# Weight maxima spread over the partitions by TensorE transposes instead of by GpSimd

## The chip, the cores and the metric

The kernel is one program on one core of a Trainium2 chip. The metric is the device time of one execution in microseconds; less is better. TensorE does the matrix products, VectorE (DVE) and ScalarE (ACT) the elementwise work and the reductions along a row, GpSimd (POOL) some elementwise work, and SyncE (SP) issues most of the transfers. A tensor in the on-chip memory has 128 partitions (rows); a reduction along a row is ordinary work for DVE, one over the partitions is not.

## The reference

One layer with two parallel branches on the normalised input, added to the input:

```python
xn = layernorm(x)                       # x: 4 sequences x 2048 x 512
# linear attention, 64 heads of 8
q = softmax(exp(beta) * heads(xn @ Wq.T + bq)); k = softmax(exp(beta) * heads(xn @ Wk.T + bk))
v = heads(xn @ Wv.T + bv)
kv = cumsum(einsum('zsD,zsd->zsDd', k, v)); kn = cumsum(k)
att = (einsum('zsD,zsDd->zsd', q, kv) / sum(q * kn)) @ Wo.T + bo
# one product whose inputs are rounded to fp8 (e4m3)
ffn = dequantised(fp8(clip(xn / input_scale))) @ (weight_fp8 * weight_scale).T + bias
out = x + att + ffn
```

## The kernel before

The 2048 positions are cut into 64 steps of 32 positions of all four sequences, which fill 128 partitions. Every engine runs its own list of work, in order, and waits on semaphores for the others. In iteration i of the main loop (`body`) TensorE makes keys, queries and values of step i, scores and attention of step i-1 and the output product of step i-2. A product in single precision is made of three in half precision: each of the five weight matrices is kept as a high part and a low part in float16 (`w_hi`, `w_lo`), scaled by a power of two that comes from the largest absolute value of the matrix.

The setup ahead of the loop makes these parts, in the order K, Q, V, F (the fp8 product's), O:

- SP loads the weights; DVE takes the largest absolute value of each partition (`largest`, L823, into one column of `amax`). GpSimd takes the maximum over the partitions and leaves it in all of them (`partition_all_reduce`, L444 for K, Q and V, L447 for F and O, into `amax_all`). DVE turns it into powers of two (`powers`, L828 to L832, `w_mult` at L867), and counts `mult_ready`.
- TensorE transposes each matrix in four chunks of four 128x128 transposes (`transpose_weights`, L1107) into seven banks of PSUM. ACT writes the high part of a chunk (`high_parts`, L567), DVE the low part (`low_parts`, L839), and then the bank is free for a later chunk.
- ACT issues the loads of the five biases at L587 (`b_loaded`). GpSimd, after both `b_loaded` and `mult_ready`, scales the biases (L453 for K and Q, which counts `bias_ready`, L456 for V) and adds the two output biases (L460, `obias_ready`).
- TensorE primes two banks (L1118, `primed`); ACT then writes the biases into the banks of keys and queries (L595, L596); only then may TensorE start keys and queries of step 0, `keys(0)` and `queries(0)`.
- Inside iteration 0, behind `queries(0)`, stand the transposes of F and O (`late_weights`, on TensorE, ACT and DVE), and behind them `values(0)`. At its end ACT sums the absolute low part of F (L581, `lo_summed`), GpSimd shares the result over the partitions (L462, `lo_total`), and TensorE reads it before iteration 2: if it is zero, as it is for a weight that is exact in fp8, every step leaves out four products with the low part of F.

At the end of iteration i ACT writes the biases for the keys of i+1 (L547, L550). The input of step i+1 is normalised by DVE (L645), split by ACT and GpSimd (L479, L402) and transposed by a transfer of SP (L324) into `xT`. In iteration 1 (`fold`) DVE adds a folded bias at L808 before `values(1)` may start; `shift` (L670, L674) is DVE's first work on the keys. On SP the load of the input of step 4 is queued behind the transposing transfers of step 1.

Of the kernel before, what the change touches and what calls it, by code (L numbers as in the profile page):

```python
# [27 lines left out]
ALU = mybir.AluOpType  # L28
ACT = mybir.ActivationFunctionType
AX = mybir.AxisListType  # L30

P = 128
# [26 lines left out]
MATRICES = 5  # L59
# [63 lines left out]
def build(nc, x, wq, bq, wk, bk, wv, bv, wo, bo, beta, wf, bf, in_scale, w_scale, const, out):  # L123
# [3 lines left out]
    with ExitStack() as ctx:  # L127
        def sb(name, shape, dt=F32):
            return ctx.enter_context(nc.sbuf_tensor(name, shape, dt))
# [4 lines left out]
        def sem(name):  # L134
            return ctx.enter_context(nc.semaphore(name))
# [26 lines left out]
        lo_sum, lo_total = sb("lo_sum", [P, 1]), sb("lo_total", [P, 1])  # L162

# [70 lines left out]
        amax_ready, amax_shared = sem("amax_ready"), sem("amax_shared")  # L234
        chain = sem("chain")
# [133 lines left out]
        def _(pool):  # L369
# [67 lines left out]
            for n in range(2):  # L437
# [5 lines left out]
            pool.wait_ge(amax_ready, 3)  # L443
            gp.partition_all_reduce(amax_all[:, 0:MO], amax[:, 0:MO], P, bass.bass_isa.ReduceOp.max)\  # L444
                .then_inc(amax_shared, 1)
            pool.wait_ge(amax_ready, MATRICES)
            gp.partition_all_reduce(amax_all[:, MO:], amax[:, MO:], P, bass.bass_isa.ReduceOp.max)\  # L447
                .then_inc(amax_shared, 1)

            pool.wait_ge(b_loaded, 16 * 5)  # L450
            pool.wait_ge(mult_ready, 1)
            for m in (MK, MQ):
# [8 lines left out]
            pool.wait_ge(lo_summed, 1)  # L461
            gp.partition_all_reduce(lo_total[:, :], lo_sum[:, :], P, bass.bass_isa.ReduceOp.max)\  # L462
                .then_inc(lo_shared, 1)
# [139 lines left out]
        def _(dve):  # L603
# [168 lines left out]
            def body(i, last_weights=None, fold=False):  # L772
# [33 lines left out]
                if fold:  # L806
                    dve.wait_ge(bvo_done, 1)
                    v.scalar_tensor_tensor(bias[:, 3, :], vo_ps[:, :], out_dn[:, :], bias[:, 3, :],  # L808
                                           ALU.mult, ALU.add).then_inc(fold_ready, 1)
# [11 lines left out]
            def largest(m):  # L821
                dve.wait_ge(w_loaded[m], 16)
                v.tensor_reduce(amax[:, m:m + 1], w_nat[m][:, :, :], AX.XY, ALU.max,  # L823
                                apply_absolute_value=True).then_inc(amax_ready, 1)

# [21 lines left out]

# [16 lines left out]
            quantise(Step(0, 0))  # L864
            dve.wait_ge(amax_shared, 1)
            powers(slice(0, MO))
            v.tensor_copy(w_mult[:, 0:MO], w_scale_up[:, 0:MO]).then_inc(mult_ready, 1)  # L867
            dve.wait_ge(mult_ready, 1)
            largest(MF)
            low_parts(MK)  # L870
            largest(MO)
            low_parts(MQ)
            low_parts(MV)
            dve.wait_ge(amax_shared, 2)
            link(v.tensor_tensor(amax_all[:, MF:], amax_all[:, MF:], abs_scales[:, :], ALU.mult))
# [12 lines left out]
            dve.wait_ge(obias_ready, 1)  # L888
# [7 lines left out]
        def _(pe):  # L896
# [195 lines left out]
            def transpose_weights(m):  # L1092

                if m == MO:
                    pe.wait_ge(wo_ordered, 1)
                else:
                    pe.wait_ge(w_loaded[m], 16)
                for c in range(KC):
                    n = turn.index(m) * KC + c
                    if last_in_bank(n) is not None:  # L1100
                        pe.wait_ge(wl_ready, last_in_bank(n) + 1)
                    for oc in range(KC):
                        src = (wo_sorted if m == MO else w_nat[m])[:, oc, c * P:(c + 1) * P]
                        dst = bank_of(n)[:, oc * P:(oc + 1) * P]
                        if m == MV:
                            dst = bank_of(n).rearrange("p (g q u f) -> p q u g f", g=GP, q=KC, f=J * DH)[:, oc]
                        last = transpose(dst, src, ident)  # L1107
                    last.then_inc(wt_done, 1)

            def late_weights():  # L1110
                transpose_weights(MF)
                transpose_weights(MO)

# [48 lines left out]
```

## Time and profile before

| | |
|---|---|
| time, median of 3 runs (lowest to highest) | 1186.12 us (1186.01 to 1186.84) |
| time of the profiled execution | 1187.5 us |
| span of that execution, first to last instruction | 1185.7 us |
| mean granted clock of TensorE | 0.982 |
| busy: TensorE, VectorE, ScalarE, GpSimd | 94%, 82%, 76%, 39% |

A profile shows one execution. Busy time is given for each engine; idle time of an engine is put down to what released the instruction behind it ("issue" is time in which the profile shows nothing that it waited for). The setup and the first two iterations take the first 101 of the 1185.7 us; the rest is the steady loop.

### The profile page before, as it was taken

To read this page: it belongs to the slowest core of one execution; us is meant where nothing else is said; L and a number is where in the kernel's file an instruction comes from. 1 tells how busy PE (TensorE), PEld (TensorE's weight loads), DVE (VectorE), ACT (ScalarE), POOL (GpSimd) and SP (SyncE) were. 2 spreads that over 40 slices of the span, in tenths; PEclk is the share of its full clock that TensorE was granted. 3 is DMA by queue.
4 is the path that set the end of the run, shared out by engine and by line. 5 is a ranking of instruction groups with operands and counts; after the bars stand their busy time and mean duration, and the time that the engine had idled before them with its cause. 6 is when DMAs were issued, how large, how long until landed. Compare 5 with 4: busy or idle time off the path is not lost.

```text
span 1185.7 us, 57406 instructions
## 1 busy us (share of the span) xinstructions
PE 1115.6 (94%) x24098; PEld 627.9 (53%) x24098; DVE 967.9 (82%) x1968; ACT 899.3 (76%) x1933; POOL 463.6 (39%) x717
## 2 busy tenths in 40 slices
PE   1458999999999999999999999999999999999996
PEld 1224555555555555555555555555555555555553
DVE  4648888888888888888888888888888888888883
ACT  0356787888878787878888888878887878787873
POOL 3133434443433444444434443443434443434420
PEclk9689999999999999999999999999999999999999
DMA  8312434544554455445445554454333343333331
GB/s 242 27 43 69 93 87 91 87 97 87 81 94 91 87 84 97 92 82 87 95 88 86 92 95 85 81 98 93 85 83 94 88 89 86 97 87 86 73 76 48
DMA packets 156468, 104.38 MB, mean 88 GB/s; under 512 B 111968, under 2 KB 128480, under 8 KB 156256
## 3 DMA queue, kind: packets, MB, share of 16 engines
q1 hardware_dynamic: 155536, 99.76, 41.1%
q8 instruction: 193, 3.16, 1.1%
q10 hardware_dynamic: 720, 1.31, 0.3%
q14 instruction: 19, 0.16, 0.0%
HBM read 40.20 MB, written 16.78 MB: 48 GB/s over the span
## 4 chain that ended last, share of the span: by engine, by line
PE 91%; issue 4%; DVE 2%; DMA 2%; POOL 1%; SPq 0%; ACT 0%; POOLq 0%; DVEq 0%
PE s_ps L941 11%; PE a_ps L1045 7%; PE vo_ps L907 5%; PE k_ps L1001 5%; PE k_ps L907 5%; PE k_ps L918 5%; PE k_ps L922 5%; PE k_ps L920 5%; PE vo_ps L911 5%; PE vo_ps L909 5%; PE q_ps L909 5%; PE q_ps L911 5%; PE k_ps L911 5%; PE k_ps L909 5%; PE q_ps L907 5%; PE a_ps L1030 4%
## 5 line engine op out<-in xcount | busy, mean ns | idle before, releaser
L496 ACT ACTIVATE st_pairs<-st_run 32x144 f32<-32x144 f32 x1008 | 331.0, 328 | 11.9
L422 POOL TENSOR_TENSOR w_own<-vp,cst 128x576 f32<-128x576 f32 x126 | 141.9, 1147 | 314.0 <-DVE vp L754 314.0
L556 ACT ACTIVATE q_heads<-qT,cst 128x512 f32<-128x512 f32 x256 | 164.1, 711 | 4.9 <-DVE qT L770 3.8
L698 DVE TENSOR_TENSOR att<-s_ps,cst 128x512 f32<-128x512 f32 x256 | 163.5, 680 | 0.3 <-PE s_ps L941 0.3
L941 PE MATMUL s_ps<-q_heads,w_own 64*64 64x128 f32 x4096 | 141.6, 275 | 1.3 <-DVE att L698 1.3
L409 POOL TENSOR_TENSOR y_sum<-y,y_magic 128x512 f32<-128x512 f32 x64 | 81.6, 1274 | 151.6 <-DVE y_magic L656 151.6
L941 PEld LDWEIGHTS s_ps<-q_heads,w_own 64*64 64x64 f32 x4096 | 110.6, 132 | 55.2 <-issue 55.0
L538 ACT ACTIVATE w_own<-kT,cst 128x512 f32<-128x512 f32 x128 | 85.5, 715 | 61.3 <-DVE kT L738 61.3
L402 POOL TENSOR_TENSOR x_split<-xn,x_split 128x512 f16<-128x512 f32 x64 | 74.6, 1165 | 137.6 <-ACT x_split L479 130.4
L479 ACT ACTIVATE x_split<-xn 128x512 f16<-128x512 f32 x64 | 40.3, 630 | 99.2 <-DVE xn L645 99.2
L907 PE MATMUL k_ps<-w_hi,xT 128*128 128x512 f16 x256 | 99.0, 387 | 17.1 <-DMA xT<-x_split 12.3
L907 PE MATMUL vo_ps<-w_hi,xT 128*128 128x512 f16 x256 | 97.7, 382 | 1.2 <-DVE bias L808 1.2
L909 PE MATMUL k_ps<-w_lo,xT 128*128 128x512 f16 x256 | 98.2, 384 | 0.0
L911 PE MATMUL k_ps<-w_hi,xT 128*128 128x512 f16 x256 | 98.0, 383 | 0.0
L918 PE MATMUL k_ps<-w_hi,ah 128*128 128x512 f16 x256 | 97.0, 379 | 0.6 <-DVE al L761 0.6
L754 DVE TENSOR_TENSOR vp<-vo_ps,vp 128x512 f32<-128x512 f32 x64 | 44.3, 692 | 64.7 <-PE vo_ps L911 64.7
L909 PE MATMUL q_ps<-w_lo,xT 128*128 128x512 f16 x256 | 97.0, 379 | 0.0
L911 PE MATMUL q_ps<-w_hi,xT 128*128 128x512 f16 x256 | 97.0, 379 | 0.0
L907 PE MATMUL q_ps<-w_hi,xT 128*128 128x512 f16 x256 | 97.0, 379 | 0.0
L909 PE MATMUL vo_ps<-w_lo,xT 128*128 128x512 f16 x256 | 97.0, 379 | 0.0
L911 PE MATMUL vo_ps<-w_hi,xT 128*128 128x512 f16 x256 | 97.0, 379 | 0.0
L922 PE MATMUL k_ps<-w_hi,al 128*128 128x512 f16 x256 | 97.0, 379 | 0.0
(144 smaller groups left out, 2272.6 us busy)
## 6 DMA issues: line engine op xcount, KB each, us to landing
v_groups<-vp SPq DMA_DIRECT2D x512, 36.0 KB, 3.3
x_in<-L_attn_x SPq DMA_DIRECT2D x64, 256.0 KB
x_res<-L_attn_x SPq DMA_DIRECT2D x64, 256.0 KB
out<-o_sb SPq DMA_DIRECT2D x64, 256.0 KB
w_own<-L_attn_Wk SPq DMA_DIRECT2D x1, 1024.0 KB, 12.7
w_own<-L_attn_Wq SPq DMA_DIRECT2D x1, 1024.0 KB, 14.7
w_own<-L_attn_Wv SPq DMA_DIRECT2D x1, 1024.0 KB, 16.5
att<-L_ffn_weight_fp SPq DMA_DIRECT2D x1, 1024.0 KB, 18.2
```

The lines of the kernel that those rows point to most:

```text
L422: last = gp.tensor_tensor(v_pairs[:, c].rearrange("p h w -> p (h w)"), vp[:, t.parity].rearrange("p h w -> p (h w)"), pair_mask[:, c:c + 1 ...
L496: last = sc.activation(st_pairs[TOK * b:TOK * (b + 1), to, u::J, :, b % SP, :], st_run[TOK * u:TOK * (u + 1), b // SP, :, b % SP, :, :], A ...
L538: last = sc.activation(k_pairs[:, i.parity, :, c, :], kT[:, :, :], ACT.Copy, scale=pair_mask[:, c:c + 1])
L556: last = sc.activation(q_heads[:, i.parity, :, j, :], qT[:, i.parity, :, :], ACT.Copy, scale=head_mask[:, j:j + 1])
L698: v.tensor_tensor(att[:, c % 2, 4 * (c // 2):4 * (c // 2) + 4, :, :] .rearrange("p g j s -> p (g j) s"), s_ps[:, DM * (c % 2):DM * (c % 2 ...
L907: mm(bank[:, :], xT[:, t.parity, 0, c, :], w_hi[:, m, c, :], start=(c == 0 and not seeded), stop=False, skip_group_check=seeded)
L909: mm(bank[:, :], xT[:, t.parity, 0, c, :], w_lo[:, m, c, :], start=False, stop=False, skip_group_check=seeded)
L911: last = mm(bank[:, :], xT[:, t.parity, 1, c, :], w_hi[:, m, c, :], start=False, stop=(c == KC - 1), skip_group_check=seeded)
L918: mm(bank[:, :], ah[:, j, :], w_hi[:, MO, j, :], start=(j == 0 and not rest), stop=False, skip_group_check=rest)
L922: last = mm(bank[:, :], al[:, j, :], w_hi[:, MO, j, :], start=False, stop=(j == J - 1), skip_group_check=rest)
L941: last = mm(s_ps[SP * TOK * gp:SP * TOK * (gp + 1), DM * n + P * q:DM * n + P * (q + 1)], k_pairs[rows, t.parity, g, :, :].rearrange("p c ...
L1045: last = mm(a_rows[TOK * u:TOK * (u + 1), n, h, :, j, :], att[:, n, J * h + u, j, :], v_groups[:, t.parity, :, n, J * h + u, j, :], start= ...
```

## The change

The three uses of `partition_all_reduce` on GpSimd go. For the weights, TensorE transposes the n columns of `amax` into n rows of `t_ps`, DVE takes the maximum of each row and writes it 128 times into a row (`spread_top`), and TensorE transposes back (`turn_top`), so that each partition has all n maxima; DVE copies them to `amax_all`. The first exchange stands on TensorE ahead of the eighth chunk of the transposes of Q, on DVE behind `quantise(0)`. The second stands on TensorE at the head of `late_weights`, behind `queries(0)`; on DVE at the place of the old wait, now behind the two maxima of F and O, which are moved behind all low parts of K, Q and V. The sum of the low parts is transposed into a row of partition 0 at the end of `late_weights`, and DVE takes its maximum (`largest_low`). DVE's wait for the added output biases is moved from before iteration 0 to L808 in iteration 1.

```diff
--- before.py
+++ after.py
@@ -160,6 +160,7 @@
         up_product = sb("up_product", [P, 1])
         lo_abs = w_own[2][:, 0:KC // 2, :].rearrange("p c d -> p (c d)").bitcast(F16)
         lo_sum, lo_total = sb("lo_sum", [P, 1]), sb("lo_total", [P, 1])
+        top, top_row = sb("top", [P, 1]), sb("top_row", [P, P])
 
         x_in = sb("x_in", [P, SLOTS, DM])
         x_res = sb("x_res", [P, 2, DM])
@@ -232,6 +233,7 @@
         c_loaded, b_loaded, m_loaded = sem("c_loaded"), sem("b_loaded"), sem("m_loaded")
         w_loaded = [sem(f"w_loaded{n}") for n in range(MATRICES)]
         amax_ready, amax_shared = sem("amax_ready"), sem("amax_shared")
+        amax_turned, top_spread, lo_turned = sem("amax_turned"), sem("top_spread"), sem("lo_turned")
         chain = sem("chain")
         mult_ready, beta_exped, in_inv_ready = sem("mult_ready"), sem("beta_exped"), sem("in_inv_ready")
         wo_ordered, lo_summed, lo_shared = sem("wo_ordered"), sem("lo_summed"), sem("lo_shared")
@@ -440,13 +442,6 @@
             root(Step(0, 0))
             low_input(Step(0, 0))
             rounding(Step(0, 0))
-            pool.wait_ge(amax_ready, 3)
-            gp.partition_all_reduce(amax_all[:, 0:MO], amax[:, 0:MO], P, bass.bass_isa.ReduceOp.max)\
-                .then_inc(amax_shared, 1)
-            pool.wait_ge(amax_ready, MATRICES)
-            gp.partition_all_reduce(amax_all[:, MO:], amax[:, MO:], P, bass.bass_isa.ReduceOp.max)\
-                .then_inc(amax_shared, 1)
-
             pool.wait_ge(b_loaded, 16 * 5)
             pool.wait_ge(mult_ready, 1)
             for m in (MK, MQ):
@@ -458,9 +453,6 @@
                              w_scale_up[:, MV:MV + 1, None, None].to_broadcast([P, J, 2, DM // J // 2]), ALU.mult)\
                 .then_inc(bias_ready, 1)
             gp.tensor_tensor(bias[:, 3, :], bias[:, 3, :], bias[:, 4, :], ALU.add).then_inc(obias_ready, 1)
-            pool.wait_ge(lo_summed, 1)
-            gp.partition_all_reduce(lo_total[:, :], lo_sum[:, :], P, bass.bass_isa.ReduceOp.max)\
-                .then_inc(lo_shared, 1)
             iterations(pool, body)
 
 
@@ -805,6 +797,7 @@
                     mask_scores(t, 3)
                 if fold:
                     dve.wait_ge(bvo_done, 1)
+                    dve.wait_ge(obias_ready, 1)
                     v.scalar_tensor_tensor(bias[:, 3, :], vo_ps[:, :], out_dn[:, :], bias[:, 3, :],
                                            ALU.mult, ALU.add).then_inc(fold_ready, 1)
                 if d.exists():
@@ -823,6 +816,17 @@
                 v.tensor_reduce(amax[:, m:m + 1], w_nat[m][:, :, :], AX.XY, ALU.max,
                                 apply_absolute_value=True).then_inc(amax_ready, 1)
 
+            def spread_top(n, done):
+
+                dve.wait_ge(amax_turned, done)
+                link(v.tensor_reduce(top[0:n, :], t_ps[0:n, 0:P], AX.X, ALU.max))
+                v.tensor_copy(top_row[0:n, :], top[0:n, 0:1].to_broadcast([n, P])).then_inc(top_spread, 1)
+
+            def largest_low():
+
+                dve.wait_ge(lo_turned, 1)
+                v.tensor_reduce(lo_total[0:1, :], t_ps[0:1, 0:P], AX.X, ALU.max).then_inc(lo_shared, 1)
+
             def powers(part):
 
                 link(v.tensor_scalar(amax_all[:, part], amax_all[:, part], 1e-18, 1e18, ALU.max, ALU.min))
@@ -844,7 +848,7 @@
                 dve.wait_ge(mult_ready, 2)
                 low_parts(MF)
                 low_parts(MO)
-
+                largest_low()
 
             dve.wait_ge(m_loaded, 48)
             link(v.reciprocal(in_rec[:, :], scal[:, 1:2]))
@@ -862,16 +866,20 @@
             magic(Step(0, 0))
             largest(MV)
             quantise(Step(0, 0))
+            spread_top(MO, 1)
             dve.wait_ge(amax_shared, 1)
+            link(v.tensor_copy(amax_all[:, 0:MO], t_ps[:, P:P + MO]))
             powers(slice(0, MO))
             v.tensor_copy(w_mult[:, 0:MO], w_scale_up[:, 0:MO]).then_inc(mult_ready, 1)
             dve.wait_ge(mult_ready, 1)
-            largest(MF)
             low_parts(MK)
-            largest(MO)
             low_parts(MQ)
             low_parts(MV)
+            largest(MF)
+            largest(MO)
+            spread_top(MATRICES - MO, 2)
             dve.wait_ge(amax_shared, 2)
+            link(v.tensor_copy(amax_all[:, MO:], t_ps[:, P:P + MATRICES - MO]))
             link(v.tensor_tensor(amax_all[:, MF:], amax_all[:, MF:], abs_scales[:, :], ALU.mult))
             powers(slice(MO, MATRICES))
 
@@ -885,7 +893,6 @@
             link(v.tensor_tensor(q_exp_scale[:, :], exp_beta[:, :], w_scale_dn[:, MQ:MQ + 1], ALU.mult))
             link(v.tensor_tensor(k_exp_scale[:, :], exp_beta[:, :], w_scale_dn[:, MK:MK + 1], ALU.mult))
             dve.wait_ge(c_loaded, 16)
-            dve.wait_ge(obias_ready, 1)
             statistics(Step(0, 2))
             body(Step(0, 0), last_weights=late_weights)
             body(Step(0, 1), fold=True)
@@ -1097,6 +1104,8 @@
                     pe.wait_ge(w_loaded[m], 16)
                 for c in range(KC):
                     n = turn.index(m) * KC + c
+                    if last_in_bank(n) == 0:
+                        turn_top(slice(0, MO), MO, 1)
                     if last_in_bank(n) is not None:
                         pe.wait_ge(wl_ready, last_in_bank(n) + 1)
                     for oc in range(KC):
@@ -1107,9 +1116,20 @@
                         last = transpose(dst, src, ident)
                     last.then_inc(wt_done, 1)
 
+            def turn_top(part, ready, done):
+
+                n = part.stop - part.start
+                pe.wait_ge(amax_ready, ready)
+                transpose(t_ps[0:n, 0:P], amax[:, part], ident).then_inc(amax_turned, 1)
+                pe.wait_ge(top_spread, done)
+                transpose(t_ps[:, P:P + n], top_row[0:n, :], ident[0:n, 0:n]).then_inc(amax_shared, 1)
+
             def late_weights():
+                turn_top(slice(MO, MATRICES), MATRICES, 2)
                 transpose_weights(MF)
                 transpose_weights(MO)
+                pe.wait_ge(lo_summed, 1)
+                transpose(t_ps[0:1, 0:P], lo_sum[:, :], ident).then_inc(lo_turned, 1)
 
             pe.wait_ge(c_loaded, 16)
             for m in (MK, MQ, MV):
```

## Rows read from the trace of the kernel before

**Rows 1.** Windows: stretch, length, busy PE, PEld, DVE, ACT, POOL (instructions), clock, DMA, GB/s.
```profile
118.40:136.00 17.60, 17.60 (x397) 9.84 (x383) 14.75 (x30) 13.94 (x31) 5.92 (x6) 1.00 0.40 87
```

**Rows 2.** Timeline of POOL: start, length (us), instruction, idle time before it and releaser.
```profile
32.71 0.38 POOL L444 PARTITION_ALL_REDUCE amax_all<-amax  x1 [7.36 <-issue]
41.37 0.37 POOL L447 PARTITION_ALL_REDUCE amax_all<-amax  x1 [8.27 <-DVE amax L823]
48.51 2.03 POOL L453 TENSOR_TENSOR bias<-bias,w_scale_up 128x512 f32<-128x512 f32 x2 [6.77 <-issue]
...
67.08 0.38 POOL L462 PARTITION_ALL_REDUCE lo_total<-lo_sum  x1 [14.32 <-ACT w_own L581]
74.74 1.14 POOL L402 TENSOR_TENSOR x_split<-xn,x_split 128x512 f16<-128x512 f32 x1 [7.28 <-issue]
```

**Rows 3.** Timeline of DVE in the setup, 25 to 54 us.
```profile
25.39 0.43 DVE L664 TENSOR_SCALAR xq_rows<-y_round 128x512 f16<-128x512 f32 x1 [0.59 <-POOL y_round L413]
33.13 0.17 DVE L828 TENSOR_SCALAR amax_all<-amax_all 128x3 f32<-128x3 f32 x1 [7.32 <-POOL amax_all L444]
...
34.15 2.29 DVE L823 TENSOR_REDUCE amax<-att 128x1 f32<-128x2048 f32 x1
36.36 0.74 DVE L839 SCALAR_TENSOR_TENSOR w_lo<-q_ps,w_mult,w_hi 128x512 f16<-128x512 f32 x1
...
46.45 0.15 DVE L875 TENSOR_TENSOR amax_all<-amax_all,abs_scales 128x1 f32<-128x1 f32 x1
...
48.48 1.08 DVE L886 TENSOR_TENSOR k_exp_scale<-exp_beta,w_scale_dn 128x1 f32<-128x1 f32 x1
53.39 0.69 DVE L619 BATCH_NORM_STATS2 stats<-x_in 128x6 f32<-128x512 f32 x1 [3.83 <-POOL bias L460]
```

**Rows 4.** Timeline of the DMA issues of ACT and SP, 21 to 34 us.
```profile
21.61 11.70 SPq L324 DMA_TRANSPOSE xT<-x_split  x1
...
24.10 0.45 ACTq L587 DMA_DIRECT2D bias<-L_ffn_bias  x1
```

**Rows 5.** Transfers, 20 to 40 us: the last number is us from issue to landing.
```profile
bias<-L_ffn_bias ACTq DMA_DIRECT2D x1, 256.0 KB, 12.8
xT<-x_split SPq DMA_TRANSPOSE x1, 16.2
```

**Rows 6.** Timeline of PE, 51 to 80 us.
```profile
51.38 0.58 PE L907 MATMUL k_ps<-w_hi,xT 128*128 128x512 f16 x1 [3.76 <-ACT k_ps L595]
...
58.14 1.04 PE L1107 MATMUL s_ps<-cst,att 128*128 128x128 f32 x8
...
64.17 0.38 PE L907 MATMUL vo_ps<-w_hi,xT 128*128 128x512 f16 x1
...
66.54 0.38 PE L911 MATMUL vo_ps<-w_hi,xT 128*128 128x512 f16 x1
79.19 0.61 PE L907 MATMUL k_ps<-w_hi,xT 128*128 128x512 f16 x1 [12.28 <-DMA xT<-x_split]
```

**Rows 7.** Timeline of ACT: the biases written for keys of step 0 and of step 1.
```profile
50.63 0.60 ACT L595 ACTIVATE k_ps<-bias 128x512 f32<-128x512 f32 x1 [7.27 <-POOL bias L453]
...
70.48 0.58 ACT L550 ACTIVATE k_ps<-bias 128x512 f32<-128x512 f32 x1
```

**Rows 8.** Timeline of DVE in iterations 0 and 1, 66 to 96 us.
```profile
66.17 0.67 DVE L726 TENSOR_REDUCE k_sum<-k_e 128x64 f32<-128x512 f32 x1
...
84.73 0.69 DVE L619 BATCH_NORM_STATS2 stats<-x_in 128x6 f32<-128x512 f32 x1 [3.87 <-DMA x_in<-L_attn_x]
...
86.26 0.68 DVE L670 TENSOR_REDUCE k_max<-k_ps 128x64 f32<-128x512 f32 x1
...
95.15 0.74 DVE L808 SCALAR_TENSOR_TENSOR bias<-vo_ps,out_dn,bias 128x512 f32<-128x512 f32 x1
```

**Rows 9.** Windows in which PE did nothing, after transposes and after products.
```profile
42.64:46.59 3.95, 0.00 (x1) 0.01 (x1) 3.95 (x7) 0.69 (x1) 0.00 (x0) 0.72 0.00 0
...
66.92:71.60 4.68, 0.00 (x0) 0.00 (x0) 3.06 (x5) 3.59 (x7) 0.38 (x1) 1.00 0.00 0
```

## The prediction

> **What bounds the kernel now.** I read the page first, for the share of each engine; then windows of a late and of an early stretch; then the timeline of each engine over the first 100 us; then the transfers. In the loop TensorE is the bound: in a window of 17.6 us, about one step, it is busy for all of it, while DVE has 14.75 and ACT 13.94 [rows 1]. So what happens ahead of the loop moves the end by as much as it moves TensorE's continuous run, no more and no less. That run begins at about 101 us; before it TensorE mostly waits. The question is thus what delays `keys(0)`, `keys(1)` and `values(1)`.
>
> GpSimd's timeline shows a pattern. The reduction over the partitions itself has a record of 0.37 to 0.38 us. But 7.36 us with nothing to wait for stand before the first, 6.77 us stand between the second and the scaling of the biases, and 7.28 us between the third and `x_split` of step 1 [rows 2]. The second has no such gap before it: it starts at 41.37, as soon as DVE's maximum of O is there. The gap comes where GpSimd changes from elementwise work to the reduction or back, not at each reduction. (Before the third the change had time inside the 14.32 us of waiting.) The second is over long before its gap ends, since DVE uses its result at 46.45 without having waited [rows 3]. I read the gaps as the loading of code for the reduction and back.
>
> The Trainium skill (GPSIMD Engine Reference, Instruction dispatch) says that the first call to a freshly loaded kernel pays about 6 us without a visible instruction. The trace agrees roughly, with 6.77 to 7.36 us; with the page's figure the first gap would be some 1.4 us shorter.
>
> Each gap has a victim. The first holds DVE's powers until 33.13 [rows 3]. The second holds the biases until 48.51, so that ACT writes the keys' bias at 50.63 [rows 7] and `keys(0)` starts at 51.38 [rows 6]. The third holds `x_split` until 74.74, so that the transposed input reaches TensorE only at 79.19, after 12.28 us of idling [rows 6]; the load of x for step 4 is queued behind it on SP, and DVE waits another 3.87 us for that [rows 8].
>
> **First exchange.** DVE begins `spread_top` behind `quantise(0)`, at 25.39 + 0.43 = 25.8 [rows 3]; the first transpose is done by then, since the maximum of V is. Neither a maximum of [n, 128] nor a single transpose is in the trace. Bounds for DVE's two operations on a row of 128: above 0.16 (the 128x1 rows), below 0.68 (the 512-wide maximum in rows 8); I take 0.3 each, a quarter of the streaming part over the fixed part. For a transpose: eight of them take 1.04 us [rows 6], so one is above 0.13 and below 1.04; I take 0.3. With a copy of 0.17 and four handovers of about 0.1 (DVE hands its step to itself in 0.03, ACT hands to TensorE in 51.38 - 51.23 = 0.15), the part behind the first transpose is 0.3 + 0.3 + 0.3 + 0.17 + 0.3 = 1.35 us, with bounds of 0.8 and 2.7. So the powers start at 27.15 instead of 33.13, and `mult_ready` comes at about 28.15. DVE's low parts start one high part later, 28.9, and are no longer broken up by the maxima of F and O (2.29 us each); 12 at a step of 0.66 (0.74 less the overlap of their records) end at 36.9. Priming takes until 37.8 (two products at half clock).
>
> **The biases.** GpSimd needs the last bias load, issued at 24.10 and landed 12.8 later, at 36.9 [rows 4, 5]. Two scalings of together 2.03 us end at 38.95, against 50.54: 11.6 us earlier. The transposed input of step 0 is there at 21.61 + 16.2 = 37.8 [rows 4, 5]. So `keys(0)` starts at 39.8 instead of 51.38, limited by the bias load; the first exchange has a slack of some 1.2 us and costs nothing here.
>
> **Second exchange.** The moved maxima end at 36.9 + 2 x 2.2 = 41.3, earlier than TensorE can use them. Here the change adds a wait: on TensorE `turn_top` stands behind `queries(0)`, where the transposes of F stood at 58.14; that is now 46.55. DVE stands still from 41.3 until then, with the powers, the statistics and `shift(0)` queued behind, and ACT waits for those. Transpose 0.35 and the chain of 1.35 give 48.3; that work started at 46.45 before, so here 1.85 us are lost. From there to the end of `k_exp_scale` it is 2.03 + 0.16 (the 1.08 of that row coincided with GpSimd's bias work, which is over by then), so statistics start at 50.55 instead of 53.39, where DVE had waited 3.83 us for the biases. That wait is moved to L808, where it has been met for 40 us. Net so far: -2.8 us on DVE and ACT, through all of the split of F and O.
>
> **The low sum.** `lo_summed` was there at about 67.0 [rows 2] and is now at 64.2. TensorE waits for it before `values(0)`, DVE before `key_sums`, which could have started at 66.17 - 2.8 = 63.4 [rows 8]. Transpose and maximum with handovers 0.75: `key_sums` at 64.95, or -1.2. The bias for the keys of step 1 ended at 71.06 [rows 7]; now at 69.85. `x_split` of step 1 no longer waits for GpSimd; from its start to TensorE it was 79.19 - 74.74 = 4.45 us, and it can begin about 54, so the input is ready near 59. `keys(1)` starts at 70.0 instead of 79.19: -9.2.
>
> **Iteration 1.** Before, DVE began `shift(1)` only at 86.26, late because of x of step 4, and was then busy without a pause up to the folded bias at 95.15 + 0.74 = 95.89, for which `values(1)` waited; so this path is DVE's 9.63 us behind the keys [rows 8]. Now x of step 4 is loaded by about 64, DVE has done its statistics by 72.2, and `shift(1)` waits for the keys. Their 12 products took 4.0 us before, since TensorE began at half clock after a pause (0.61 us for the first); at full clock they take 12 x 0.215 = 2.6 (11 steps in 66.54 - 64.17) [rows 6]. The pause before them is now 2.8 us, from 67.2 to 70.0. In an idle stretch of 4.68 us after these very products the clock stayed at 1.00; in one of 3.95 us after transposes it fell, mean 0.72 [rows 9]. I take the former. Keys end at 72.65, the folded bias at 82.4, against 95.89: **-13.5 us**. At half clock it is -12.1. Behind that TensorE is continuous, but for the same branch, so the loop keeps it. I forecast -13.4.
>
> The profiled execution took 1187.5 us for a span of 1185.7, and gives 1187.5 - 13.4 = 1174.1. It is 1.4 above the median; from the median it is 1186.12 - 13.4 = **1172.7**.
>
> **Rivals.**
> 1. `keys(1)` at half clock: -12.1, 1174.0. Chance 0.22; the shorter pause speaks against it, the sparse work before it for it.
> 2. The biases are usable before 36.9 (their transfer may be held up by GpSimd's code loading, which ends at 32.7): then priming limits, and `keys(0)` moves by another 1.2, 1171.5. Chance 0.10.
> 3. DVE doesn't catch up in iteration 1, because x of step 4 is late again or the second exchange takes its upper bound: then only the shift of `keys(1)` counts, -9.2, 1176.9. Chance 0.12.
> 4. The gaps are not the reductions' but come with GpSimd's resuming work, and stay. Then biases at 36.9 + 6.8 give `keys(0)` at 46.6, the second exchange ends at 55.1, 8.65 later than 46.45, statistics at 57.35 (+4.0), the keys' bias of step 1 at 71.06 + 4.0 + 1.55 = 76.6; `keys(1)` gains 2.6: 1183.5. Against it is the second reduction, which had no gap after 8.27 us of idling. Chance 0.05. The Trainium skill (GPSIMD Engine Reference, Engine selection) puts a reduction over partitions on GpSimd. In this case that would hold only if the gaps stay; the 0.38 us of the record is indeed less than the exchange.
> 5. Slower: the low sum in partition 0 becomes something other than an exact zero, so TensorE takes the other branch. That is decided by one bit, and adds 4 products in each of 64 steps: 4 x 64 x 0.215 = 55 us, 1228. A transpose of zeros, with maxima over them, gives zero. Chance 0.02.
> 6. No difference, or a small loss by pauses of the loop that begin with another phase of DVE and TensorE: 1186, chance 0.04, of which 0.01 slower.
>
> **How the numbers follow.** The forecast's own chance is 0.45. Rivals 1, 2 and 3 with it make 0.89. The range reaches from 1171.0, rival 2 with half a microsecond for the lower bound of the exchange, to 1177.3, rival 3 with as much above; rivals 4 to 6 are outside. A change of 0.2% (2.4 us) is about what a measurement can tell from none. Faster: forecast and rivals 1 to 4, 0.94; the same 0.03; slower 0.03.
>
> **What would show it.** Right: no idle "issue" time of 7 us on GpSimd; biases at 37; `keys(0)` near 40 and `keys(1)` near 70; a wait of DVE of 5 us or more for TensorE in the second exchange; statistics at 50.5; the folded bias near 82.4; 17.2 to 17.6 us per step later. Wrong: any 7-us gap on GpSimd, a bias load after 38, a clock of half in `keys(1)`, DVE waiting for x of step 4, a TensorE window with pauses after 90 us, or eight instead of four fp8 products in a step.

## The result

| | before | changed |
|---|---|---|
| median, lowest to highest | 1186.48 us (1186.01 to 1187.94) | 1174.94 us (1173.30 to 1177.18) |
| profiled execution, its span | 1187.5 us, 1185.7 us | 1173.3 us, 1171.5 us |

The ratio is 0.990, with a 95% interval of 0.9888 to 0.9912: 11.5 us, or 1.0%, faster. The forecast was 1172.7 with a range of 1171.0 to 1177.3. A second measurement of the same changed kernel gave 1174.87 against 1187.64, a ratio of 0.9891 (0.9876 to 0.9906).

These are lines of the changed kernel's page of the profile; TensorE's busy time is the 1116 us of before, give or take two, in a span that is 14 us shorter.

```profile
span 1171.5 us, 57412 instructions
## 1 busy us (share of the span) xinstructions
PE 1117.6 (95%) x24103; PEld 629.9 (54%) x24103; DVE 969.3 (83%) x1975; ACT 898.9 (77%) x1933; POOL 462.8 (40%) x714
```

The changed kernel's timeline of GpSimd. The answers to [rows 2] are the biases at 36.86, released by the last bias load and no longer by a gap of 6.77 us, and `x_split` of step 1 at 54.13, released by ACT.

```profile
23.96 1.27 POOL L415 TENSOR_TENSOR y_round<-y_sum,y_magic 128x512 f32<-128x512 f32 x1
36.86 2.04 POOL L448 TENSOR_TENSOR bias<-bias,w_scale_up 128x512 f32<-128x512 f32 x2 [11.63 <-DMA bias<-L_ffn_bias]
...
54.13 1.16 POOL L404 TENSOR_TENSOR x_split<-xn,x_split 128x512 f16<-128x512 f32 x1 [13.02 <-ACT x_split L471]
```

The changed kernel's timeline of DVE, against [rows 3] and [rows 8]: the first exchange, the last maximum, the second exchange with the wait of 6.58 us ahead of it, the statistics, the maximum of the low sum with its wait of 1.57 us, and in iteration 1 `shift` and the folded bias.

```profile
25.61 0.27 DVE L822 TENSOR_REDUCE top<-t_ps 3x1 f32<-3x128 f32 x1
25.91 0.21 DVE L823 COPY top_row<-top 3x128 f32<-3x128 f32 x1
26.48 0.16 DVE L871 COPY amax_all<-t_ps 128x3 f32<-128x3 f32 x1 [0.36 <-PE t_ps L1125]
26.68 0.17 DVE L832 TENSOR_SCALAR amax_all<-amax_all 128x3 f32<-128x3 f32 x1
...
38.60 2.27 DVE L816 TENSOR_REDUCE amax<-q_heads 128x1 f32<-128x2048 f32 x1
47.45 0.28 DVE L822 TENSOR_REDUCE top<-t_ps 2x1 f32<-2x128 f32 x1 [6.58 <-PE t_ps L1123]
...
48.50 0.16 DVE L883 TENSOR_TENSOR amax_all<-amax_all,abs_scales 128x1 f32<-128x1 f32 x1
...
50.74 0.69 DVE L611 BATCH_NORM_STATS2 stats<-x_in 128x6 f32<-128x512 f32 x1
...
65.85 0.28 DVE L828 TENSOR_REDUCE lo_total<-t_ps 1x1 f32<-1x128 f32 x1 [1.57 <-PE t_ps L1132]
66.06 0.66 DVE L718 TENSOR_REDUCE k_sum<-k_e 128x64 f32<-128x512 f32 x1
...
73.87 0.69 DVE L662 TENSOR_REDUCE k_max<-k_ps 128x64 f32<-128x512 f32 x1 [0.77 <-PE k_ps L918]
...
82.77 0.74 DVE L801 SCALAR_TENSOR_TENSOR bias<-vo_ps,out_dn,bias 128x512 f32<-128x512 f32 x1
```

And TensorE's, against [rows 6]: `keys(0)`, the second exchange, the transposes of O with 8.97 us of idling before them, the transpose of the low sum, `values(0)` and `keys(1)`.

```profile
39.73 0.58 PE L914 MATMUL k_ps<-w_hi,xT 128*128 128x512 f16 x1 [2.58 <-ACT k_ps L587]
...
47.15 0.27 PE L1123 MATMUL t_ps<-cst,amax 128*2 128x128 f32 x1
...
59.12 1.94 PE L1116 MATMUL s_ps<-cst,w_own 128*128 128x128 f32 x8 [8.97 <-DVE w_lo L843]
60.86 1.91 PE L1116 MATMUL a_ps<-cst,w_own 128*128 128x128 f32 x8
65.44 0.37 PE L1132 MATMUL t_ps<-cst,lo_sum 128*1 128x128 f32 x1 [2.67 <-ACT w_own L573]
65.61 0.63 PE L914 MATMUL vo_ps<-w_hi,xT 128*128 128x512 f16 x1
...
71.08 0.38 PE L914 MATMUL k_ps<-w_hi,xT 128*128 128x512 f16 x1 [1.45 <-ACT k_ps L542]
```

The reader is to see two things. The three gaps of GpSimd are gone, and what stood behind them now starts at 36.86 (48.51 before) and 54.13 (74.74 before). And TensorE's work is not all at full clock where the prediction had it so: eight transposes of O take 1.94 us, where eight of F took 1.04 in [rows 6] and the same eight of O 1.22 in the kernel before, and the first product of `values(0)` 0.63 instead of 0.38.

Where the time came from can be followed by marks. The folded bias ends at 83.51, against 95.89: 12.4 us earlier. The first output is written by DVE at 101.00, against 113.37: 12.4. The 16th is 13.9 earlier, and the 64th 14.1. In the second profile of the same kernel the 1st, 16th and 64th output were 12.3, 13.8 and 13.3 earlier. The setup accounts for 12.3 to 12.4 us in both; what the loop adds differs by up to a microsecond between these two profiles (14.1 and 13.3 at the 64th output).

### The profile page after: what moved, and what is told of

Its sections match the earlier page's. It is cut to its first block, busy times and chain, and to the rows that moved or that the text cites. A ratio compares the mean times of both kernels' runs of the same rounds, so it can differ in the third digit from the quotient of the medians.

```text
span 1171.5 us, 57412 instructions
## 1 busy us (share of the span) xinstructions
PE 1117.6 (95%) x24103; PEld 629.9 (54%) x24103; DVE 969.3 (83%) x1975; ACT 898.9 (77%) x1933; POOL 462.8 (40%) x714
## 4 chain that ended last, share of the span: by engine, by line
PE 93%; DMA 2%; DVE 2%; ACT 1%; issue 1%; SPq 0%; POOL 0%; ACTq 0%; DVEq 0%
PE s_ps L948 11%; PE a_ps L1052 7%; PE k_ps L914 5%; PE vo_ps L914 5%; PE k_ps L1008 5%; PE k_ps L916 5%; PE k_ps L918 5%; PE k_ps L925 5%; PE k_ps L927 5%; PE k_ps L929 5%; PE q_ps L916 5%; PE vo_ps L918 5%; PE q_ps L918 5%; PE vo_ps L916 5%; PE q_ps L914 5%; PE a_ps L1037 4%
```

## The experiments

The kernels of each group were timed in turns with the kernel before on one chip. The ratio is to the kernel before, with its 95% interval. The kernel before had a median of 1187.64 us in the group of repeat, two_unused, low_gpsimd and second_gpsimd, 1187.67 in that of first_only to order_early, 1187.46 in that of low_later and all_early, and 1186.72 in that of the last two. Kernels of different groups are therefore compared by what they gained on the kernel before of their own group; for the repeat that is 12.8 us. The starts (us) are from the profile of each: `keys(0)`, the statistics behind the second exchange, `key_sums`, `keys(1)`, `shift(1)` on DVE, the folded bias.

| kernel | median | ratio | keys(0) | statistics | key_sums | keys(1) | shift(1) | folded bias |
|---|---|---|---|---|---|---|---|---|
| before | 1186.48 | 1 | 51.38 | 53.39 | 66.17 | 79.19 | 86.26 | 95.15 |
| changed | 1174.94 | 0.990 (0.9888 to 0.9912) | 39.73 | 50.74 | 66.06 | 71.08 | 73.87 | 82.77 |
| repeat | 1174.87 | 0.9891 (0.9876 to 0.9906) | 39.68 | 51.14 | 66.16 | 71.19 | 73.98 | 82.88 |
| two_unused | 1178.54 | 0.9919 (0.9904 to 0.9935) | 43.16 | 53.84 | 69.17 | 74.20 | 77.06 | 85.97 |
| low_gpsimd | 1185.32 | 0.9975 (0.9966 to 0.9984) | 40.25 | 51.23 | 64.70 | 78.28 | 85.31 | 94.21 |
| second_gpsimd | 1178.36 | 0.9919 (0.9904 to 0.9933) | 51.95 | 44.14 | 68.42 | 73.45 | 77.87 | 86.77 |
| first_only | 1181.59 | 0.9951 (0.9937 to 0.9964) | 45.64 | 47.22 | 60.01 | 72.44 | 80.12 | 89.02 |
| maxima_early | 1176.51 | 0.9905 (0.9890 to 0.9920) | 42.38 | 53.38 | 68.70 | 73.73 | 76.52 | 85.42 |
| exchange_early | 1171.79 | 0.9867 (0.9852 to 0.9882) | 40.07 | 48.62 | 63.95 | 68.97 | 71.76 | 80.66 |
| order_early | 1170.42 | 0.9855 (0.9840 to 0.9870) | 39.61 | 48.31 | 61.66 | 66.69 | 69.48 | 78.38 |
| low_later | 1173.92 | 0.9886 (0.9869 to 0.9902) | 39.75 | 51.06 | 64.52 | 69.56 | 72.59 | 81.48 |
| all_early | 1169.58 | 0.9853 (0.9836 to 0.9869) | 41.35 | 48.98 | 60.63 | 65.67 | 68.71 | 77.59 |
| bias_split | 1171.67 | 0.9877 (0.9862 to 0.9893) | 38.22 | 48.66 | 63.99 | 69.01 | 71.80 | 80.70 |
| all_and_split | 1168.04 | 0.9842 (0.9829 to 0.9855) | 38.90 | 47.62 | 59.22 | 64.26 | 68.74 | 77.63 |

The theory: GpSimd spends about 7 us on a change between elementwise work and a reduction over the partitions, and the change gains by taking these off the path, that is, out of the chain of waits that decides when the loop starts. The rivals: each reduction costs 7 us; the gaps are not the reductions'; one of the three is all of the gain.

**repeat.** The changed kernel once more, as a control.

> The changed kernel once more, beside the others of its group: 11 to 14 us less than before. If the 1.7 us by which its first profile gained more than the 12.4 us present at the first output was chance, a second profile shows another difference inside the loop, with the same 12.4 us at its head.

As expected: 12.8 us below the kernel before in its group, 12.3 at the first output.

**two_unused.** The changed kernel with two reductions whose results nobody uses.

```diff
+            pool.wait_ge(amax_ready, MO)
+            for s in spare:
+                gp.partition_all_reduce(s[:, :], amax[:, 0:MO], P, bass.bass_isa.ReduceOp.max)
             pool.wait_ge(b_loaded, 16 * 5)
```

> The changed kernel with two reductions over the partitions on GpSimd, one right behind the other, whose results nobody uses, started at about 25 us. Theory (GpSimd loads code when it changes from elementwise work to a reduction or back): a gap of about 7.4 us before the first, none before the second, one of about 6.8 us behind it, so the biases start at 40.3 instead of 36.86 and the time is 3.4 us above the changed kernel. Rival (each reduction has its own gap of 7 us): biases at 47, 10 us above. Second rival (the gaps belong to waits of the kernel before, not to reductions): no gap, time as changed.

GpSimd's timeline in this kernel:

```profile
24.14 1.26 POOL L416 TENSOR_TENSOR y_round<-y_sum,y_magic 128x512 f32<-128x512 f32 x1
32.72 0.74 POOL L448 PARTITION_ALL_REDUCE spare<-amax  x2 [7.31 <-issue]
40.29 2.03 POOL L452 TENSOR_TENSOR bias<-bias,w_scale_up 128x512 f32<-128x512 f32 x2 [6.82 <-DMA xT<-x_split]
```

Both reductions stand in one row, 0.74 us in all, with one gap of 7.31 before and one of 6.82 behind. (The row names a transfer as the releaser of the second gap, but the biases don't wait for that one.) The biases start at 40.29, as forecast to a hundredth, and the time is 3.7 us above the repeat's. That rules out the first two rivals: a gap belongs to a change of kind, and it comes with reductions that serve no purpose. How well the numbers agree is in part luck. In this profile the last bias load, issued at 24.22, took 15.3 us instead of 12.8 and was there only at about 39.5, so by itself it would have held the biases to within 0.8 us of 40.29. That the way back to elementwise work costs 7 us whatever the loads do is seen more clearly in the kernel before, where that load had been there for 11 us when the biases started behind a gap of 6.77 [rows 2]. That the gap is code being loaded is a reading and isn't shown; no transfer shows in the trace in the gap from 41.8 to 48.5 of the kernel before.

**low_gpsimd.** The low sum on GpSimd again.

```diff
+            pool.wait_ge(lo_summed, 1)
+            gp.partition_all_reduce(lo_total[:, :], lo_sum[:, :], P, bass.bass_isa.ReduceOp.max)\
+                .then_inc(lo_shared, 1)
             iterations(pool, body)
...
-                largest_low()
...
-                pe.wait_ge(lo_summed, 1)
-                transpose(t_ps[0:1, 0:P], lo_sum[:, :], ident).then_inc(lo_turned, 1)
```

> The changed kernel with the low sum shared by GpSimd again, the rest on TensorE. Theory: the reduction itself at about 65.5, then a gap of 7.2 us, x_split of step 1 at 73, keys(1) at 77.5 instead of 71.1, x of step 4 late, the folded bias about 10.5 us later: time 9 to 11 us above the changed kernel, only 1 to 3 below the kernel before. Rival (the third reduction is hidden and only DVE's and TensorE's waits for it go): 1 to 2 us below the changed kernel.

```profile
66.02 0.38 POOL L457 PARTITION_ALL_REDUCE lo_total<-lo_sum  x1 [24.39 <-ACT w_own L576]
73.76 1.14 POOL L404 TENSOR_TENSOR x_split<-xn,x_split 128x512 f16<-128x512 f32 x1 [7.35 <-issue]
...
83.79 0.69 DVE L614 BATCH_NORM_STATS2 stats<-x_in 128x6 f32<-128x512 f32 x1 [3.83 <-DMA x_in<-L_attn_x]
```

10.4 us above the repeat. The table shows how: `key_sums` is even earlier (64.70), `keys(1)` is 7 us later, and `shift(1)` is 11 us later, since x of step 4 is queued behind the late `x_split` and DVE waits 3.83 us for it. Of the two reductions that were put back one at a time this one, of a single number for each partition, cost the most: 10.4 us, against 3.5 for that of F and O in the next experiment.

**second_gpsimd.** The maxima of F and O on GpSimd again.

```diff
+            pool.wait_ge(amax_ready, MATRICES)
+            gp.partition_all_reduce(amax_all[:, MO:], amax[:, MO:], P, bass.bass_isa.ReduceOp.max)\
+                .then_inc(amax_shared, 1)
             pool.wait_ge(b_loaded, 16 * 5)
...
-            spread_top(MATRICES - MO, 2)
             dve.wait_ge(amax_shared, 2)
-            link(v.tensor_copy(amax_all[:, MO:], t_ps[:, P:P + MATRICES - MO]))
...
-                turn_top(slice(MO, MATRICES), MATRICES, 2)
```

> The changed kernel with the maxima of F and O shared by GpSimd again, ahead of the biases. Theory: the reduction at 41, its gap until 48, keys(0) at 51, 11 us later than in the changed kernel; but DVE no longer stands behind queries(0) for the exchange, it only waits for the keys, shift(0) about 55.2 instead of 53.3, and the transposes of O are no longer at half clock: 0.5 to 2 us above the changed kernel. Rival (keys(0) sets the end, as my prediction chained it): 8 to 11 us above.

3.5 us above the repeat, above the theory's 2 and far below the rival's 8. `keys(0)` is 12.3 us later, but the statistics are 7 us earlier, as DVE has no exchange to wait for, and `keys(1)` is only 2.3 later. Another 1.6 us come from the clock, in TensorE's timeline of this kernel:

```profile
62.70 1.22 PE L1117 MATMUL s_ps<-cst,w_own 128*128 128x128 f32 x8 [1.53 <-DVE w_lo L846]
...
68.02 0.38 PE L915 MATMUL vo_ps<-w_hi,xT 128*128 128x512 f16 x1
...
73.45 0.59 PE L915 MATMUL k_ps<-w_hi,xT 128*128 128x512 f16 x1 [2.68 <-ACT k_ps L545]
```

Here the transposes of O follow after 1.53 us of idling and are at full clock, so is `values(0)`, and `keys(1)` is at half clock after 2.68 us of idling. In the changed kernel it is the reverse. `shift(1)` thus comes 4.4 us behind the start of `keys(1)`, not 2.8. This kernel keeps the maxima of F and O where the change put them, behind the low parts, so GpSimd's reduction starts at 41.25 here. It doesn't tell what that reduction costs where DVE takes these maxima early; first_only does.

**first_only.** The kernel before with the first exchange on TensorE alone; on DVE and TensorE it is written as in the change.

```diff
-            pool.wait_ge(amax_ready, 3)
-            gp.partition_all_reduce(amax_all[:, 0:MO], amax[:, 0:MO], P, bass.bass_isa.ReduceOp.max)\
-                .then_inc(amax_shared, 1)
```

> The kernel before with the first exchange (K, Q, V) on TensorE and nothing else changed. Theory: the maximum of O is reached at about 34.8 instead of 41.3, the second reduction and its gap move along, biases done at 44, keys(0) at 44.9 instead of 51.4, and the rest keeps that: 6 to 6.5 us below the kernel before. Rival (the first gap is off the path, since the biases are the bound): no difference.

6.1 us below the kernel before, as the theory had it. The reduction of F and O starts at 35.43 instead of 41.37 and the biases at 42.77 instead of 48.51. So with two reductions left the first one's gap was on the path through the maximum of O, which stood behind it on DVE.

```profile
55.63 1.22 PE L1115 MATMUL s_ps<-cst,w_own 128*128 128x128 f32 x8 [1.53 <-DVE w_lo L838]
...
60.01 0.68 DVE L725 TENSOR_REDUCE k_sum<-k_e 128x64 f32<-128x512 f32 x1
```

There is more in these rows. With the reduction of F and O left on GpSimd, and its gap of 6.96 us, the statistics (47.22) are 3.5 us earlier than in the changed kernel and `key_sums` (60.01) 6.1 us, because DVE has no exchange to wait for and the transposes of O run at full clock. Only the third gap then holds `keys(1)` until 72.44, after 11.68 us of idling.

**maxima_early.** The maxima of F and O back among the low parts.

```diff
+            largest(MF)
             low_parts(MK)
+            largest(MO)
             low_parts(MQ)
             low_parts(MV)
-            largest(MF)
-            largest(MO)
```

> The changed kernel with the maxima of F and O back at their old places among the low parts. Theory: the last low part ends at 40.8 instead of 36.4, priming limits, keys(0) at 42.5 instead of 39.7, and the second exchange behind queries(0) moves with it: 2.8 us above the changed kernel. Rival (the late maxima don't matter): same time.

In the trace `keys(0)` is 2.65 us later than in the changed kernel and everything up to the folded bias stays 2.6 later. The time is 1.6 us above, with an interval that overlaps the repeat's, where 2.8 were expected. `keys(0)` follows TensorE's priming here (0.78 us of idling behind it), although the last bias load was late too and held the biases until 38.35. The trace shows the mechanism, the timing alone doesn't separate the two.

**exchange_early.** The second exchange between `keys(0)` and `queries(0)`.

```diff
+                if last_weights:
+                    turn_top(slice(MO, MATRICES), MATRICES, 2)
                 if i.exists():
                     queries(i)
...
-                turn_top(slice(MO, MATRICES), MATRICES, 2)
                 transpose_weights(MF)
```

> The changed kernel with the second exchange on TensorE between keys(0) and queries(0). Theory (DVE's 6.6 us of waiting behind queries(0) is on the path): the exchange at 44.8 instead of 47.4, statistics 2.6 us earlier, queries(0) 0.9 later, which nobody needs before 67: 2 to 2.6 us below the changed kernel. Rival (that wait is hidden, TensorE's work is what counts): same or 0.9 us above.

DVE's timeline in this kernel:

```profile
45.34 0.28 DVE L822 TENSOR_REDUCE top<-t_ps 2x1 f32<-2x128 f32 x1 [4.05 <-PE t_ps L1125]
```

3.1 us below the repeat and below the first measurement of the changed kernel by as much; the marks from the statistics on are 2.1 us earlier. The interval overlaps the repeat's by 0.0006 and is clear of that of the first measurement. So DVE's wait behind `queries(0)` was on the path; the marks show 2.1 of the 3.1 us.

**order_early.** In addition ACT puts O in order behind the first biases.

```diff
             sc.activation(q_ps[:, :], bias[:, MQ, :], ACT.Copy).then_inc(qseed_ready, 1)
+            order_wo()
             body(Step(0, 0), last_weights=late_weights)
```

> As exchange_early, and ACT puts the columns of O in order (2.2 us) right behind the first biases, where it idles, instead of ahead of the high parts of F. Theory: DVE's low parts of F start 1.7 us earlier still, 3.5 to 4.3 us below the changed kernel. Rival (the transposes of O at half clock, after 9 us of TensorE idling, set the pace whatever ACT does): no gain over exchange_early.

TensorE's timeline in this kernel, at the transposes of O:

```profile
54.89 1.88 PE L1121 MATMUL s_ps<-cst,w_own 128*128 128x128 f32 x8 [4.62 <-DVE w_lo L846]
56.56 1.91 PE L1121 MATMUL a_ps<-cst,w_own 128*128 128x128 f32 x8
```

From `key_sums` on the marks are 2.3 us earlier than in exchange_early, of which 0.3 were there at the statistics already; the rest is somewhat more than the 1.7 expected. The median is 1.4 lower and the intervals overlap; against the repeat it is 4.5, just above the 3.5 to 4.3 expected. The pause before the transposes is 4.62 instead of 8.97 us and they are at half clock all the same, so this cost stays, and the ordering is a cost of its own.

**low_later.** The low sum behind `values(0)`; TensorE's transposes of the V bias wait for `lo_shared`.

```diff
-                pe.wait_ge(lo_summed, 1)
-                transpose(t_ps[0:1, 0:P], lo_sum[:, :], ident).then_inc(lo_turned, 1)
...
             body(Step(0, 0), last_weights=late_weights)
+            turn_low()
             body(Step(0, 1), fold=True)
```

> The changed kernel with the transpose of the low sum behind values(0) on TensorE, and its maximum on DVE at the end of iteration 0. Theory: DVE's wait of 1.57 us ahead of key_sums goes, key_sums at 64.3 instead of 66.06, keys(1) 1.7 us earlier: 1.5 to 1.8 us below the changed kernel. Rival (keys(1) is limited by something else, such as the clock): same time.

`key_sums` is at 64.52, 1.5 us earlier, and so is `keys(1)`; 1.3 remain at the folded bias. It gained 13.5 us on the kernel before of its group, 0.8 more than the repeat, where 1.5 to 1.8 were expected, and the intervals overlap: the marks agree with the theory, the timing doesn't settle it.

**all_early.** The last three together.

> exchange_early, the early ordering of O and the late low sum together. Theory: the three gains add, 5 to 6 us below the changed kernel, 17 below the kernel before. Rival: they overlap in one wait, and it is 4 or less.

17.9 us below the kernel before in its group, 5.1 more than the repeat: the three gains add, as expected. In its profile the biases started at 38.47, released by the last bias load, and not at 36.8, so `keys(0)` was 1.6 late; from `keys(1)` on the marks were still the earliest so far (`key_sums` was earlier in first_only).

**bias_split.** The changed kernel with the biases of K and Q no longer waiting for the other three loads.

```diff
-            pool.wait_ge(b_loaded, 16 * 5)
+            pool.wait_ge(kq_loaded, 16 * 2)
             pool.wait_ge(mult_ready, 1)
...
+            pool.wait_ge(b_loaded, 16 * 3)
             gp.tensor_tensor(bv_sorted.rearrange(...
```

> The changed kernel, but GpSimd scales the biases of K and Q as soon as these two are loaded (about 28 us) and waits for the other three only behind them. Theory (keys(0) waits for the last bias load at 36.9): keys(0) now waits for priming and the transposed input at 37.9, so it starts at 38.0 to 38.7 instead of 39.7; the second exchange and all behind it move along, 1.0 to 1.7 us below the changed kernel. Rival (TensorE, at half clock from an earlier or a later moment, or DVE's late maxima at 40.9 take it back): same time.

```profile
29.59 2.04 POOL L449 TENSOR_TENSOR bias<-bias,w_scale_up 128x512 f32<-128x512 f32 x2 [4.51 <-DMA bias<-L_attn_bk]
36.47 1.04 POOL L453 TENSOR_TENSOR o_sb<-bias,w_scale_up 128x512 f32<-128x512 f32 x1 [4.84 <-DMA bias<-L_ffn_bias]
```

`keys(0)` starts at 38.22, 1.5 us earlier, then limited by priming. TensorE also reached full clock after 8 of its 12 products, not after 11, and the statistics are 2.1 earlier, which lasts to the folded bias. It gained 15.1 us on the kernel before of its group, 2.3 more than the repeat, with intervals that overlap. That is more than the 1.0 to 1.7 expected and agrees with the 2.1 of the marks. The medians themselves are 3.2 apart, but the kernel before was 0.9 faster in this group too.

**all_and_split.** all_early with the same edit.

> all_early with the split bias wait. Theory: the exchange between keys(0) and queries(0) is released by the end of keys(0) near 42.7, which is still behind DVE's last maximum at 40.9, so 1 to 2 us below all_early, more where a run of all_early got its last bias late (38.5 in its profile). Rival: no gain beyond all_early.

1168.04 us is the lowest of all; its interval overlaps that of all_early. It gained 18.7 us on the kernel before of its group, 0.8 more than all_early, where 1 to 2 were expected. Its profile shows why the 1.4 us at `keys(1)` didn't last. The granted clock was 1.00 through the whole pause of 3.53 us and in the first product, and 0.59 over 64.40 to 65.00: it fell after the work had begun again.

```profile
64.26 0.38 PE L919 MATMUL k_ps<-w_hi,xT 128*128 128x512 f16 x1 [3.53 <-ACT k_ps L544]
64.48 0.59 PE L921 MATMUL k_ps<-w_lo,xT 128*128 128x512 f16 x1
64.86 0.64 PE L923 MATMUL k_ps<-w_hi,xT 128*128 128x512 f16 x1
```

`shift(1)` and the folded bias come at 68.74 and 77.63, where all_early had 68.71 and 77.59.

**What each reduction was worth.** Against the kernel before of its own group, taking the first reduction off GpSimd gained 6.1 us (first_only), the first and the second 2.3 (low_gpsimd), the first and the third 9.3 (second_gpsimd), and all three 12.8 (repeat). So no single one is all of the gain, and the shares don't add up. As long as the third gap stood, taking the second reduction away, with the maxima moved for it, made the kernel 3.8 us slower (low_gpsimd against first_only). It is thus not shown that the second exchange is a gain where the change puts it. The kernel that would tell was not run: the first exchange and the low sum on TensorE, the second reduction on GpSimd and its maxima early. An estimate from rows: the transposes of O start at 55.63 in first_only, in second_gpsimd `key_sums` follows that start by 68.42 - 62.70 = 5.72 us, and `keys(1)` follows `key_sums` by 5.02 in the changed kernel. Together that is 66.4 for `keys(1)`, against 71.08 in the changed kernel.

## Why the prediction was right, step by step

**The gaps** were read rightly, and two_unused shows it: the price is for a change of kind, 6.8 to 7.5 us each time. The Trainium skill (GPSIMD Engine Reference, Instruction dispatch) has about 6 us for the first call to a freshly loaded kernel; all gaps here are longer, and one of the same size stands on the way back to elementwise work. The Trainium skill (GPSIMD Engine Reference, Engine selection) gives a reduction over partitions to GpSimd. That didn't hold for these reductions of one to three columns: an exchange took 1.07 us behind its first transpose, against 0.38 for the reduction plus its gaps.

**First exchange.** Forecast 25.8 to 27.15, measured 25.61 to 26.68; DVE's two operations took 0.27 and 0.21 (0.3 each taken), a transpose 0.22 to 0.37 (0.3 taken).

**The biases.** Forecast 36.9 and 39.8 for `keys(0)`, measured 36.86 and 39.73. That the bias load is the limit is shown by bias_split, where `keys(0)` came 1.5 us earlier. That the maxima had to move for it is seen in the trace of maxima_early.

**Second exchange.** Forecast 46.55 for the transpose and 48.3 for the powers, measured 47.15 and 48.50; statistics 50.74 for 50.55. `keys(0)` stayed at half clock for longer than before, and the shorter exchange made up for it. The wait added to DVE was 6.58 us, and exchange_early shows that it costs 2 to 3 us of the end. What the prediction didn't ask is whether this exchange should leave GpSimd at all: it compared 48.3 with the 46.45 of the kernel before, where the first gap had made DVE late with its low parts. With that gap gone and the rest left alone DVE goes on with the maxima of F and O at 40.48 (first_only).

**The split of F and O** is the step that was mis-sized. I let the gain of 2.8 us pass through it unchanged. But the transposes of F now run ahead, right behind the exchange, and those of O wait for banks that DVE can free only after ACT's work; TensorE idles for 8.97 us, where it had idled for 1.74 in the kernel before:

```profile
61.79 1.22 PE L1107 MATMUL s_ps<-cst,w_own 128*128 128x128 f32 x8 [1.74 <-DVE w_lo L839]
```

Windows of the changed kernel over this idling and over the transposes of O show what that does to the clock:

```profile
50.00:59.00 9.00, 0.16 (x2) 0.00 (x0) 6.67 (x20) 5.49 (x10) 3.43 (x3) 0.75 0.22 44
59.00:64.00 5.00, 3.65 (x16) 3.27 (x16) 4.68 (x7) 4.11 (x7) 2.56 (x13) 0.50 0.25 81
```

At a granted clock of 0.50, that is 1.2 GHz, each chunk takes 0.86 us and ACT, which needs 0.58, waits for TensorE; four chunks make 1.1 us. The low sum is ready at 65.4 instead of the forecast 64.2, and `key_sums` starts at 66.06 instead of 64.95, nearly where it was before. That 1.1 us is carried to the end: `keys(1)` 71.08 for 70.0, `shift(1)` 73.87 for 72.65, the folded bias done at 83.51 for 82.4, so 12.4 us for 13.5. In the second profile of the same kernel the last eight of the transposes took 1.51 us, with a mean clock of 0.72, and `key_sums` still came at 66.16; no run takes the half clock away and nothing else.

**keys(1)** was at full clock as forecast, but not for the reason given. The pause before it was 1.45 us, since `values(0)` itself ran at half clock at first and ended late. With a pause near the 2.8 us that I had worked out, second_gpsimd had half clock (2.68 us) and all_early full clock (2.62 us, a first product of 0.38). What I took from one row of before was a coin toss, and the row was only the first 4.68 us of an idling of 12.28: over 66.92 to 79.00 us the mean clock was 0.70, and the products behind it began at half clock. That full clock came true is luck.

**Iteration 1.** DVE did catch up: x of step 4 was there, and `shift(1)` waited 0.77 us for the keys. From `shift(1)` to the end of the folded bias it was 9.64 us, forecast 9.63. low_gpsimd shows the other side of it, with x late and 10.4 us lost.

The forecast of 1172.7 was 2.2 us too low. 1.1 of them are the half clock in the split of F and O, and 0.4 come from the kernel before, whose median was 1186.12 us when I took it and 1186.48 in the end. The rest is no larger than what two measurements of the changed kernel differ by (11.5 and 12.8 us gained); what makes executions differ isn't settled here. The mechanism was right in the gaps, the biases and iteration 1, mis-sized in the split of F and O, and right by luck in the clock of `keys(1)`.

## What to carry to other kernels

Where GpSimd alternates between elementwise work and a reduction over partitions, look for an idle time ahead of the instruction behind each change, not at the record of the reduction: 0.38 us there stood for 7 to 14 us of gaps. A maximum over partitions of a few columns costs about 1 us as two TensorE transposes with DVE between, but these stand in the queues of both engines, so place them where TensorE is free and DVE has its operand. Take the reductions one by one, and time each removal alone: here the third was worth the most, and for the second no gain over its old arrangement is shown. Before counting a shift of one engine through a stage, ask what another engine, now early, will do: a TensorE that idles may come back at half clock, as it did here after 8.97 us.

## What was not expected of the hardware

The clock after short pauses did not follow from their length. The clearest case is the priming of the two banks, which comes after 2.71 us of idling and the same transposes in the changed kernel and in its repeat:

```profile
36.55 0.39 PE L1138 MATMUL k_ps<-w_hi 128*128 128x512 f16 x1 [2.71 <-DVE w_lo L843]
...
36.86 0.61 PE L1138 MATMUL k_ps<-w_hi 128*128 128x512 f16 x1 [2.71 <-DVE w_lo L843]
```

The first row (changed) is at full clock, the second (repeat) at half: in the first the clock had risen right behind the transposes (a mean of 0.97 over 33.9 to 36.5 us), in the second it had not (0.50). Elsewhere work began at full clock after idling of 1.45, 1.53 and 2.62 us and at half clock after 2.58 (`keys(0)` of the changed kernel) and 2.68. After 3.53 us the first product was still at full clock (0.38 us) and the second was not (0.59). Transposes of O began at half clock after pauses of 4.62 and 8.97 us; in the changed kernel all 16 stayed there, in its repeat the clock rose during the last eight.

The last bias load landed 12.8 us after its issue, beside 4.3 to 5.0 us for the first three, and it varied: it held the biases until 38.35 in maxima_early and 38.47 in all_early, where the other profiles in which the biases wait for it had 36.7 to 37.4. That load, not the maxima, limited `keys(0)` in the changed kernel.
